# Attention scores of a one-core transformer kernel: nine bf16 products in 72 rows become four float32r products in 32-row tiles

## The reference

```
qkv = einsum('bsd,ed->bse', layernorm(x), qkv_w) + qkv_b     # 16 heads of 8
scores = einsum('bhqe,bhke->bhqk', q, k) * scale
attn = softmax(scores, axis=-1)
out = einsum('bhqk,bhke->bhqe', attn, v)
```

## Time and profile before

| what | value |
|---|---|
| median of three runs | 1849.06 us |
| the profiled execution, its time | 1840.17 us |
| its span, first to last instruction | 1838.4 us |
| mean granted TensorE clock | 0.928 |
| preparation (norm, projections, parts) | about 176 to 217 us |
| main block | about 217 to 996 us |
| all that follows | about 996 to 1838 us |

### The profile page before, as it was taken

The page is one execution under the profiler, slowest core; times in us unless marked ns, Lnnn a source line. Parts: engine busy times, 40 slices in busy tenths (PEclk is TensorE's granted clock), DMA queues, the critical chain, the costliest instruction groups (busy, mean ns, idle before and its releaser), DMA issues. The chain is left out here.

```text
span 1838.4 us, 21584 instructions
## 1 busy us (share of the span) xinstructions
PE 1607.5 (87%) x7285; PEld 675.5 (37%) x7285; DVE 1352.3 (74%) x1951; ACT 856.2 (47%) x1493; POOL 222.4 (12%) x145
## 2 busy tenths in 40 slices
PE   6987589999999999999998799899984446589999
PEld 3433212222222222222223344466651112266665
DVE  5775798888888888888851777556666999745554
ACT  2443417777777777777776434322223000132221
POOL 2222300000000000000000122211100334201110
PEclk8998659999999999999999999899996767799999
DMA  6000310011001100120000000000000000000000
GB/s 171 4 0 1 124 30 8 15 28 37 12 15 28 33 15 15 28 32 10 2 2 1 1 0 0 1 1 0 0 1 0 0 1 0 1 1 6 6 6 7
DMA packets 32017, 29.42 MB, mean 16 GB/s; under 512 B 7789, under 2 KB 27033, under 8 KB 31929
## 3 DMA queue, kind: packets, MB, share of 16 engines
q1 hardware_dynamic: 31928, 28.31, 6.1%
HBM read 22.13 MB, written 4.19 MB: 14 GB/s over the span
## 5 line engine op out<-in xcount | busy, mean ns | idle before, releaser
L1350 DVE TENSOR_REDUCE mx<-ps 128x1 f32<-128x1024 f32 x512 | 603.1, 1219 | 108.9 <-PE ps L1262 107.6
L1338 ACT ACTIVATE xT<-ps 128x512 f32<-128x512 f32 x512 | 277.8, 598 | 123.4 <-PE ps L1285 117.0
L1262 PE MATMUL ps<-k,q 72*128 72x512 bf16 x1024 | 324.0, 399 | 11.0 <-DVE mx L1350 9.3
L1285 PE MATMUL ps<-q,k 84*128 84x512 bf16 x1024 | 311.7, 383 | 8.9 <-ACT xT L1338 6.4
L1338 ACT ACTIVATE xn<-ps 128x512 f32<-128x512 f32 x512 | 278.1, 601 | 83.9 <-PE ps L1285 79.1
L1285 PEld LDWEIGHTS ps<-q,k 84*128 84x128 bf16 x1024 | 96.4, 97 | 372.7 <-ACT xn L1338 152.6
L854 ACT ACTIVATE silu<-ps 128x512 f32<-128x512 f32 x144 | 85.3, 596 | 265.2 <-PE ps L827 261.8
L889 DVE TENSOR_TENSOR hid<-ps,silu 128x512 f32<-128x512 f32 x144 | 97.8, 689 | 90.2 <-PE ps L831 88.5
L827 PE MATMUL ps<-xT,ew 128*128 (+1 forms) x288 | 150.4, 604 | 6.4 <-PEq L1718 4.8
L817 PEld LDWEIGHTS ps<-ew,hid 128*128 128x128 f32 x1152 | 138.7, 192 | 30.6 <-issue 29.9
L831 PE MATMUL ps<-xT,ew 128*128 (+1 forms) x288 | 148.8, 599 | 0.0
(11 more groups left out here) (239 smaller groups left out, 1686.2 us busy)
## 6 DMA issues: line engine op xcount, KB each, us to landing
k<-k_parts SPq DMA_DIRECT2D x90, 64.0 KB
q<-q_parts SPq DMA_DIRECT2D x144, 32.0 KB
k<-k_parts SPq DMA_DIRECT2D x108, 32.0 KB
ew<-in_L_ffn_w_dram SPq DMA_DIRECT2D x2, 1024.0 KB
wraw<-in_L_ffn_w_dram SPq DMA_DIRECT2D x3, 512.0 KB, 6.7
q_parts<-part SPq DMA_DIRECT2D x4, 384.0 KB, 3.9
k_parts<-part SPq DMA_DIRECT2D x4, 384.0 KB, 2.6
v<-values SPq DMA_DIRECT2D x8, 144.0 KB, 6.1
```

The costliest lines, as they stand in the source:

```text
L1262: mm = nc.tensor.matmul(m.ps[:, S1B[2 * (i % 2) + kc % 2], :], queries, k1[:, h, kc * CHUNK:(kc + 1) * CHUNK], start=True, stop=True)
L1285: nc.tensor.matmul(m.ps[:, S2B[n % len(S2B)], :], k2[:, h, kt * P:(kt + 1) * P], q[:, qc, h, :], start=True, stop=True).then_inc(s2_ready, 1)
L1338: nc.scalar.activation(ex[kt % P_RING][:, h, :], m.ps[:, S2B[n % len(S2B)], :], ACT.Exp)\
L1350: nc.vector.reduce_max(mx[:, h, qt, kc:kc + 1], m.ps[:, 2 * (i % 2):2 * (i % 2) + 2, :], AX.XY)\
```

## The change

The scores are made from two parts instead of three. The first part of a float32 is the number with its last twelve bits set to zero (`HI_BITS`, a bitwise and), the second is the rest. Both are kept in float32 width and multiplied as float32r. The 2 x 2 products of 8 rows take 32 rows per head, and the four heads of a group stand side by side in the four 32-row tiles of PE. The row r of a tile is chosen with a stride of four (`rows_of`).

- Preparation: DVE has one operation per job in place of three, ACT one in place of two, POOL has the subtraction. The first five jobs go straight from SBUF to the rows of q and k1 by four DMAs each, beside the write to DRAM.
- First pass: each matmul stands for itself, two in a slot, with heads 2 and 3 for even pairs and heads 0 and 1 for odd ones. The maximum is taken from one bank of 512 columns, 64 of them in a unit. There are three banks: the matmul n waits for the maximum n-3.
- Second pass: scores come in pairs of heads into four banks. Each pair is two matmuls of 32 rows and two of 2 rows, which add the negated maximum (`ones` by `neg_row`) in the same banks. The ones in k2, that ACT made, are gone.
- The maxima are two parts, in float32, moved by eight DMAs a unit in place of four; the chain has four operations in place of seven.
- Between the first pass of unit 0 (with the seven pairs that follow it) and the first score stand six float32 matmuls of 128 x 128 by 512 columns (`WARM`); the matmul of zeros ahead of all is gone.

```diff
-    S1B, S2B, AVB = [0, 1, 2, 3], [4, 5, 6], 7
+    S1B, S2B, AVB = [0, 1, 2], [3, 4, 5, 6], 7
...
+            def low_part(n):
+                pool.wait_ge(hi_ready, n + 1)
+                nc.gpsimd.tensor_tensor(part[:, n % PART_RING, 1, :], full[:, n % 2, :], part[:, n % PART_RING, 0, :],
+                                        ALU.subtract).then_inc(lo_ready, 1)
...
-                step(nc.vector.tensor_tensor(rest[:, :], full[:, n % 2, :], part[:, n % PART_RING, 0, :], ALU.subtract))
-                step(nc.vector.tensor_copy(part[:, n % PART_RING, 1, :], rest[:, :]))
-                nc.vector.tensor_tensor(part[:, n % PART_RING, 2, :], rest[:, :], part[:, n % PART_RING, 1, :], ALU.subtract)\
+                nc.vector.tensor_scalar(part[:, n % PART_RING, 0, :].bitcast(I32), full[:, n % 2, :].bitcast(I32), HI_BITS,
+                                        None, ALU.bitwise_and).then_inc(hi_ready, 1)
...
+            return (2, 3) if i % 2 == 0 else (0, 1)
...
-                if u > 0 or i >= 2:
-                    pe.wait_ge(s1_used, u * PAIRS + i - 1)
+                for j, h in enumerate(first_heads(i)):
+                    n = (u * PAIRS + i) * 2 + j
+                    if n >= len(S1B):
+                        pe.wait_ge(s1_used, n - len(S1B) + 1)
+                    rows = slice(h * ROW_TILE, (h + 1) * ROW_TILE)
+                    queries = q[rows, qc, :].rearrange("r (p t) -> r t p", t=TPC)[:, qt, :]
+                    nc.tensor.matmul(m.ps[:, S1B[n % len(S1B)], :], queries, k1[rows, kc * CHUNK:(kc + 1) * CHUNK],
+                                     start=True, stop=True).then_inc(s1_ready, 1)
...
-                    pe.wait_ge(exped, n - len(S2B) + 1)
-                nc.tensor.matmul(m.ps[:, S2B[n % len(S2B)], :], k2[:, h, kt * P:(kt + 1) * P], q[:, qc, h, :],
-                                 start=True, stop=True).then_inc(s2_ready, 1)
+                    pe.wait_ge(exped, n + 1 - len(S2B) + 1)
+                for k in (n, n + 1):
+                    rows = slice(k % GH * ROW_TILE, (k % GH + 1) * ROW_TILE)
+                    nc.tensor.matmul(m.ps[:, S2B[k % len(S2B)], :], k2[rows, kt * P:(kt + 1) * P], q[rows, qc, :],
+                                     start=True, stop=False)
+                for k in (n, n + 1):
+                    rows = slice(k % GH * ROW_TILE, k % GH * ROW_TILE + PARTS2)
+                    nc.tensor.matmul(m.ps[:, S2B[k % len(S2B)], :], ones[rows, :], neg_row[rows, u % 2, :],
+                                     start=False, stop=True).then_inc(s2_ready, 1)
...
+            for i in range(WARM):
+                nc.tensor.matmul(m.ps[:, AVB, :], m.projT[:, 0, :], m.w1T[:, 0:TPC, :].rearrange("p a b -> p (a b)"),
+                                 start=True, stop=True)
+            score(0)
+            score(2)
...
-                    score(n + 3)
+                    score(n + 4)
                     ahead(u, 2 * kt)
-                    score(n + 4)
-                    score(n + 5)
                     score(n + 6)
                     ahead(u, 2 * kt + 1)
                     weigh(u, kt)
...
-                    nc.vector.reduce_max(mx[:, h, qt, kc:kc + 1], m.ps[:, 2 * (i % 2):2 * (i % 2) + 2, :], AX.XY)\
-                        .then_inc(s1_used, 1)
+                    for j, h in enumerate(first_heads(i)):
+                        n = (u * PAIRS + i) * 2 + j
+                        dve.wait_ge(s1_ready, n + 1)
+                        nc.vector.reduce_max(mx[:, h, qt, kc:kc + 1], m.ps[:, S1B[n % len(S1B)], :], AX.X)\
+                            .then_inc(s1_used, 1)
```

More of the change, by code:

```diff
@@ L6 @@
 BF16 = mybir.dt.bfloat16
+F32R = mybir.dt.float32r
+I32 = mybir.dt.int32
 ALU = mybir.AluOpType
@@ L957, in softmax_attention, with rows_of @@
     zeros = m.sb("zeros", [P, CHUNK], BF16, stack=kv_stack)
[L958 to L963, removed]
+    def rows_of(tile, r):
+        return tile[r:P:ROW_BLOCKS, :].bitcast(F32)
@@ L984, in _ @@
+            nc.gpsimd.memset(ones[:, :].bitcast(F32), 1.0)
+            norm.rstds(pool, 0)
+            norm.rstds(pool, 1)
+            norm.rstds(pool, 2)
+            norm.rstds(pool, 3)
+            for n in range(len(jobs)):
+                low_part(n)
             nc.gpsimd.memset(zeros[:, :], 0.0)
@@ L1050, in _ @@
         def _(sp):
[L1051 to L1086 removed]
+            for n, (s, c) in enumerate(jobs):
+                slot = n % PART_RING
+                sp.wait_ge(lo_ready, n + 1)
+                if n < N_DIRECT:
+                    tile = q[:, 0, :] if s == 0 else k1[:, c * CHUNK:(c + 1) * CHUNK]
+                    for r in range(ROW_BLOCKS):
+                        i = r // PARTS2 if s == 0 else r % PARTS2
+                        sp.dma_start(rows_of(tile, r), part[0:GH * HD, slot, i, :]).then_inc(direct[slot], 16)
+                sp.dma_start(sides[s][2][:, :, c * CHUNK:(c + 1) * CHUNK].rearrange("i p t -> p i t"),
+                             part[:, slot, :, :]).then_inc(parts_out[slot], 16)
             for i in range(PART_RING):
[L1088 to L1089 removed]
+                sp.wait_ge(parts_out[i], 16 * len(range(i, len(jobs), PART_RING)))
+                sp.wait_ge(direct[i], 16 * ROW_BLOCKS * len(range(i, N_DIRECT, PART_RING)))
     m.stage()
@@ L1202, in load_next_q @@
                 if qc == 0:
[L1203 removed]
+                    if g > 0:
                         sp.wait_ge(s2_ready, u * STEPS)
@@ L1300, in weigh @@
                 last.then_inc(av_done, 1)
-            nc.tensor.matmul(m.ps[:, AVB, :], zeros[:, 0:P], zeros[:, :], start=True, stop=True)
             for i in range(PAIRS):
@@ L1372, in maxima @@
                 dve.wait_ge(max_turned, u + 1)
-            maxima(0, True)
-            for u in range(1, UNITS):
+            for u in range(UNITS):
                 maxima(u)
```

200 lines of the change are left out of this document (76 added, 124 removed).

## The result

| | before | after |
|---|---|---|
| median of runs | 1846.84 us (4 runs, 1841.06 to 1851.38) | 2337.42 us (4 runs, 2335.08 to 2346.34) |
| profiled execution, its time | 1840.17 us | 2337.64 us |
| span | 1838.4 us | 2335.9 us |
| mean granted TensorE clock | 0.928 | 0.692 |

The changed kernel is slower, by a ratio of 1.267 with an interval of 1.263 to 1.271. The prediction was 1873 in a range of 1785 to 2060: the direction was right, the size was not.

A forecast was written before the change was run, and what follows sets the result against it. PE was taken to bound the main block before, the three-bank wait after. Terms -6 + 3.2 - 0.6 - 0.4 + 7.1 + 26.6 - 6.2 = +23.7 us on the 1849 median gave 1873, range 1785 to 2060.

The forecast's parts named there:

- rival 3: PE's clock falls or doesn't stay up: a turn of 4.6 us, +28 a unit, about 2290 us; chance 0.08.
- The turn: Main block, x0 to next x0 through three first-pass banks: 2.97 us a key tile, +26.6 us over fourteen units.
- The boundary: Between units: 0.5 us, half of before, as the maxima's chain is shorter and DVE can catch up.
- Preparation: Block ahead of the first pass: fewer DVE operations but more bytes, ending at 211 instead of 217.0, -6 us.
- The tail: Last tiles, without a first pass: 2.05 us a tile in place of 2.38, -6.2 us.
- unit 1: Seven pairs ahead, six float32 matmuls and first scores added: 54.9 us for 47.8, +7.1.
- the new wait: Fourth first-pass matmul waits for the bank of the first: PE idles about 0.8 us in each key tile.
- the six matmuls: Float32 matmuls ahead of the first score: 7 us, lifting the clock on their way.
- rival 4: The six matmuls don't lift the clock, the mix does later: +3 to +10 us; no separate chance given.
- the eight DMAs of the maxima: Eight a unit in place of four: taken as 0, with 36 us kept for the range.
- Rival 1: Main block bound by DVE alone, 42.2 us a unit, 1787 us; chance 0.28 with what lies towards the forecast.
- rival 2: First-pass and score pairs don't run side by side, or float32r needs two passes: about 2050 or 2090 us; chance 0.13.

The follow-up runs named there:

- experiment 1: The kernel before with both passes cut to 32 rows at work, 2450.92 us; the same with 64 rows, 2444.35 us.
- experiment 2: The kernel before with idle time added, by another maximum of 512 columns ahead of each maximum: 2040.8 us.
- experiment 4: The changed kernel with full-row filler matmuls each key tile: three, unit 0 included, 2008.23 us; from unit 1 on, one 2367.78, two 2175.28, three 1975.1.
- experiment 8: The changed kernel with two or three full-row fillers a tile, maxima over 256 of 512 columns: 1931.72 and 1940.21 us, against 2175.28 and 1975.1 with whole maxima.
- experiment 6: The kernel before with 32 rows in the scores alone, the first pass keeping 72 rows: 2133.2 us.
- experiment 3: The changed kernel without the six float32 matmuls ahead of the first score (WARM = 0): 2345.98 us.
- experiment 5: The changed kernel with all 128 rows in scores and first pass, 2260.77 us; with 128 rows in the first pass alone, 2078.99 us.

## Why the prediction was wrong

**The step that failed** is the clock. Every term of the sum was taken at 1.00, and rival 3, which had the fall, got 0.08. Its "against" was that the tail of before worked 72% of the time and stayed at the full clock. That argument counted busy time. The scores of that tail had 84 rows; experiment 1 shows the clock at 0.50 with 64 rows and PE always busy, experiment 2 at 1.00 with idle time in each tile. Rival 3 did name the rows ("uses at most 64 of its rows at a time"), but with no row of the trace on either side it was given too little. Its price was near: 2290 for 2337. Its turn of 4.6 came out as 5.00. The prediction doesn't show how 4.6 is made up (the pieces it names give 0.86 + 1.25 + 0.31 + 1.71 = 4.13); measured, scores and maxima take 1.02 cold, x0 to x3 1.41, x3 with its weight load 0.74 to the weighing, and the weighing 1.83. That the price was near is in part luck.

**The sum at full clock** is short as well, +24 for +129 (experiment 4).

- The turn, 2.97 predicted, is 3.28 (experiment 8). The weighing, 0.98, was right. From x0 to the weighing it is 606.92 - 605.19 = 1.73, not 1.25 + 0.31 = 1.56: DVE starts 0.44 after x0 (0.41 predicted), the maximum of x0 ends at 605.63 + 0.68 = 606.31, the weight load of x3 starts at 606.37 and takes 0.30, and 0.25 behind its end comes the weighing. The record of x3 starts with that load, at 606.37. I had 0.10 for the load, with ends of 0 and 0.2. Scores and maxima take 605.19 - 604.62 = 0.57, not 0.43: 0.33 for the scores (504.72 to 505.05 with half maxima) and 0.24 for the maxima. Sixteen tiles of 0.31 more are 5.0 a unit.
- The boundary is 54.3 - 16 x 3.28 = 1.8, not 0.5. It lies in two places of the kernel with three fillers. The tile ahead of the empty slot has two pairs of the first pass in one slot and takes 4.59 us (423.07 to 427.66), the one behind it 2.97; and the first tile of a unit takes 4.22 (386.11 to 390.33), with the four scores at two times and 0.30 of waiting for ACT. The prediction had halved the 1.0 of before with no row for it. With the tiles that is 6.3 a unit, 88 in 14.
- Preparation was to save 6 and saved 2. The timeline of its end, where the earlier trace rows had 211.89 and 217.00:

```profile
203.66 0.43 DVE L1045 TENSOR_SCALAR part<-full 128x512 int32<-128x512 int32 x1 [2.83 <-DMA k_parts<-part]
...
207.02 0.43 DVE L1045 TENSOR_SCALAR part<-full 128x512 int32<-128x512 int32 x1 [2.93 <-DMA k_parts<-part]
...
214.94 0.34 PEld L1240 LDWEIGHTS ps<-k,q 32*128 32x128 f32 x3 [15.89 <-issue]
```

  DVE, whose three operations went, waits for the DMA that frees a slot of the ring of parts; the larger bytes are what ends last.
- The tail has 2.2 to 2.3 a tile at full clock (the weighings at 1449.87, 1452.20 and 1454.40), not 2.05: +4 in 19 tiles.
- Some 9 us of the 129 are left, in unit 1, which took 64.7 us (256.62 to 321.35) for 54.9: some 5 by its longer tiles, the rest probably because it ran partly cold even with fillers (0.79 in 265 to 290).

**What was right.** The place and size of the new wait (0.77 for 0.8), DVE at 0.62 a maximum for 0.64 (2.48 us for four), the six matmuls (7.71 us for 7, and they did lift the clock, against rival 4), and 0 for the eight DMAs of the maxima: 4.34 us long, and nowhere does a row name them as what PE's scores waited for. Rival 1 (DVE the bound) and rival 2 (no overlap) are out: DVE idles, and the pairs overlap. The four matmuls of L1264, two pairs, take 0.81 us together cold (276.61), as long as one of L1240 alone (279.04), so a pair doesn't wait for the one ahead of it in other row tiles. But the four hold PE 0.33 us at full clock and a pair by itself 0.34 (273.27 to 273.61), where I took 0.215 a pair. That makes three phases of scores, maxima and first pass where I counted five, but the turn is what ends last, and this gains nothing. The Trainium skill ("TensorEngine Tiling (Array Packing)", "PSUM Bottleneck") says that reading PSUM may bound once tiling has made TensorE faster; experiment 8 agrees, with 3.28 against 3.00 us a tile.

## What to carry to other kernels

Ask of a change that packs a product into fewer rows not only how many columns PE saves, but over how many rows the matmuls of the new mix run. Here 32 or 64 rows in both passes of the kernel before halved TensorE's clock with PE always busy. In the changed kernel the low clock cost some 362 us, more than twice the 129 that the rest of the change did. Look at the granted clock in windows before explaining a longer tile, and test it with fillers of full rows in time that PE idles anyway. In a turn of a bank the weight load behind the wait counts at its full length (0.30 us here).

## What was not expected of the hardware

- In these main loops PE's being busy was not enough for the full clock: 0.50 with 32 rows (float32r or bf16) or 64 in both passes, 1.00 with 72 and 84, and 1.00 or 0.99 again with all 128 in the first pass. The weighing, over 128 rows in every one of them, did not hold it alone there, though it did in the tail of the changed kernel (1.00 in 1450 to 1470).
- The same instructions can run at either level: 0.50 and then 1.00 in one run (experiment 6), and 0.50 or 1.00 in the same tail (experiment 3).
- A weight load of 32 rows by 128 columns in float32 that stands behind a wait takes 0.30 us at full clock (606.37 in experiment 8) and as much at half of it (279.04); in the kernel before, two of 72 rows in bf16 behind a wait took 0.15 together, at half the clock (259.45).
- A pair of float32r matmuls over all 128 rows and 512 columns holds PE 0.66 us at full clock (experiment 5), where a bf16 pair over 72 rows held it 0.43. What part its weight loads have in that is not shown.
- Matmuls of 72 rows among matmuls of 32 rows take longer: 0.55 us a pair for 0.43, and a tile of 3.15 for 2.82 (experiment 6).
